# A token mixer with experts on one core: spans and exponentials of a step formed at the end of the step before, and four mixing deltas in one pass

## The chip, the cores and the metric

The kernel runs on one core of a Trainium2 chip, in float32. The metric is the device time of one execution in microseconds. Three runs of the kernel before gave 6115.89, 6119.67 and 6131.08 us; the median is 6119.67.

## The reference, cut to what matters

The first layer is a recurrent token mixer over x of shape (2, 4096, 512) with 16 heads of 32 channels; the second routes the 8192 rows to 8 experts by balanced assignment and runs a two-layer feed-forward net in each. The change touches the mixer alone.

```python
xx  = xprev - x
mix = tanh((x + xx * time_maa_x) @ time_maa_w1.T).reshape(B, T, 4, -1)
deltas = einsum('btfd,fcd->fbtc', mix, time_maa_w2)               # four of them, from 32 channels each
xrg, xwa, xk, xv = x[None] + xx[None] * (time_maa + deltas)
r = xrg @ receptance.T ; k = xk @ key_w.T ; v = xv @ value.T ; ...  # gates, decay w, kk, a, b = -kk * a
def step(S, inp):                                                 # over T, for each head, S is 32 x 32
    sab = einsum('bhvk,bhk->bhv', S, kk_)
    S = S * exp(w_)[:, :, None, :] + sab[..., None] * b_[:, :, None, :] + v_[..., None] * k_[:, :, None, :]
    y = einsum('bhvk,bhk->bhv', S, r_)
    return (S, y)
```

Then y is normed per head, a bonus is added, the gate multiplies, and `output` projects it.

## The kernel before, in words

**Tiles and chunks.** A tile is 64 tokens of each of the two sequences, 128 columns; channels lie on partitions in four groups (G). There are 64 tiles. The recurrence is solved in chunks of 32 tokens: in a chunk, queries (`kkn` and `r`) meet keys (`b` and `k2`), each weighted by an exponential of a difference of summed log-decays (`csum`). The difference is taken in blocks of 8 tokens against a reference in the block: `query_span` writes it into `dq` for all queries, `key_span(j)` into the second half of `keys` for the keys that block j can see, 128 to 512 wide (j = 0 to 3). ACT takes the exponentials in place (`exp_of_queries`, `exp_of_keys`), POOL multiplies them with `kkn` and `r` (`queries_u`, `queries_y`), DVE with `b` and `k2` (`make_keys`).

**Stages of a tile.** A tile passes five stages in successive steps: N loads its rows and norms them; A transposes x, mixes it, projects it and forms decays and keys; B forms the products of queries and keys (scores `u0` to `u5`, `y0` to `y5`), masks them into `raw`, and projects the values; C inverts the triangular systems by doubling (`inverse_stage`, k = 1, 2, 4, 8, 16), and passes the state through the two chunks; D norms, gates and projects the output. One `step` runs A of tile d + 3 and B of tile d + 2 beside C and D of older ones, so all of them are interleaved on each engine. Of 68 steps 28 are written out in a loop that runs twice, the others stand before and behind it.

**What sets the order.** The order is written by hand, one list per engine (`DVE_STEPS`, `ACT_STEPS`, `POOL_STEPS`, `PE_STEPS`, lines 255 to 274) that names every operation as stage.name, and the calls at the end of `on_vector`, `on_scalar`, `on_gpsimd` and `on_tensor` in the same order. Each operation adds one to its engine's semaphore of the step, and a consumer waits for a count (`dve["A.scan"]` of this step, `dve.ago(...)` of the step before). An engine runs its own list in order: whatever stands behind a waiting instruction waits too. Engines may run apart by less than two steps (`enter`, and `on_sync`, which issues all DMAs).

**PSUM.** Eight banks are shared in turns (`BANK`, line 275). Before a product is written, `clear` waits for the reader of the tenant before: delta0 in bank 3 follows `rated` (read by DVE as `A.rated`), delta3 in bank 2 follows `value` (read by ACT as `B.v`), score u3 follows u1 in bank 5 and u5 follows u3.

**PE's head of a step** before: transposes of x, value (0,2), first inverse stage (128 matmuls of 32 x 32), centring, mixing (needs `xxx`), router scores, value (2,3), variance, second stage (128), deltas 0 to 2, value (3,4), gate of the output, `gate1` (needs `xf0`), bonus, half of stage 4, `low_wa` (needs `xf1`), the other half, delta 3, score u0, stage 8 with `low_k` between its halves, score u1, key projection.

**Lines that matter.** L358 `query_span`, L363 `key_span`, L369 and L372 `make_keys`, L387 masks, L402 and L408 lerp and `xf`, L415 transposes between inverse stages, L426 `turn_z`, L430 to L436 the state, L443 `rated`, L504 `D.acc`, L531 the scan, L550 `xx`, L553 `xxx`; on PE L992 projections, L1001 low-rank products, L1025 inverse stages, L1040 scores, L1094 deltas, L1117 transposes of x, L1127 centring, L1134 mixing, L1188 the second low-rank pass; on POOL L902 `grow_of`, L914 `rk`.

## Time and profile before

| what | value |
|---|---|
| median of three runs | 6119.67 us |
| the profiled execution's own time | 6134.68 us |
| its span | 6132.7 us |
| PE busy | 5583.4 us (91%) |
| DVE busy | 3823.3 us (62%) |
| ACT busy | 1982.8 us (32%) |
| POOL busy | 1368.9 us (22%) |

All durations come from one profiled execution. The mixer takes the span's first 4180 us or so, the routing and the experts the rest. Busy time of PE counts matmuls from start to modelled end; a wait is put down to what released it, and "issue" stands where nothing that the profile shows did.

### The profile page before, as it was taken

How to read it: one execution, taken by the hardware profiler on the slowest of the kernel's cores; microseconds unless marked ns; L12 is line 12 of the kernel's file. 1: busy time of each engine (PE TensorE's matmuls, PEld its weight loads, DVE VectorE, ACT ScalarE, POOL GpSimd, SP SyncE). 2: the span in 40 equal slices, each digit the busy share in tenths (PEclk: the TensorE clock that was granted, in tenths of full speed). 3: DMA queues.
4: the chain of work that ended last, by engine and by line, in shares of the span. 5: the costliest groups of instructions: out<-in, count | busy, mean ns of one | idle time of the engine just before them, and what ended most of it. 6: DMA issues, size and time to landing. Idle time of an engine off the chain costs nothing. (4 is left out here: it accounts for less than half of the span.)

```text
span 6132.7 us, 244823 instructions
## 1 busy us (share of the span) xinstructions
PE 5583.4 (91%) x111176; PEld 3878.1 (63%) x111176; DVE 3823.3 (62%) x9004; ACT 1982.8 (32%) x3595; POOL 1368.9 (22%) x1156
## 2 busy tenths in 40 slices
PE   6989999898998998988999899883999999999998
PEld 5777777777777777777777777762444444444443
DVE  5887887888788787787887887874322332332310
ACT  3444444444444444444444444431100000000000
POOL 1222222222222222222222222221220220220220
PEclk9999999999999999999999999995999999999999
DMA  1000001000010000000000000003021121211210
GB/s 59 23 17 19 23 18 24 17 22 20 17 24 18 20 22 17 24 17 19 23 17 23 19 18 23 17 16 99 21 77 62 59 75 62 70 65 62 71 62 14
DMA packets 108641, 211.14 MB, mean 34 GB/s; under 512 B 25552, under 2 KB 26704, under 8 KB 107088
## 3 DMA queue, kind: packets, MB, share of 16 engines
q1 hardware_dynamic: 92240, 144.91, 8.1%
q0 software_dynamic: 15360, 50.48, 2.5%
q8 instruction: 882, 14.45, 1.0%
q14 instruction: 159, 1.30, 0.1%
HBM read 144.60 MB, written 50.72 MB: 32 GB/s over the span
## 5 line engine op out<-in xcount | busy, mean ns | idle before, releaser
L387 DVE COPY_PREDICATED time_raw<-time_known,w_bank 128x96 f32<-128x96 int32 (+6 forms) x3072 | 831.5, 275 | 337.3 <-PE w_bank L1040 245.2
L1850 PE MATMUL moe_bank<-moe_w,moe_hidden 128*128 128x512 f32 x2048 | 928.7, 596 | 0.0
L1837 PE MATMUL moe_bank<-moe_hT,moe_w 128*128 128x512 f32 x2048 | 923.4, 594 | 0.8 <-DVE moe_hT L1737 0.8
L1758 ACT ACTIVATE moe_hidden<-moe_bank,moe_b 128x512 f32<-128x512 f32 x256 | 175.9, 687 | 1628.1 <-PE moe_bank L1837 1628.1
L1837 PEld LDWEIGHTS moe_bank<-moe_hT,moe_w 128*128 128x128 f32 x2048 | 386.4, 190 | 471.3 <-issue 470.1
L1850 PEld LDWEIGHTS moe_bank<-moe_w,moe_hidden 128*128 128x128 f32 x2048 | 379.4, 190 | 429.5 <-issue 428.1
L902 POOL TENSOR_TENSOR time_grow<-time_eye,time_grow 128x512 f32<-128x512 f32 x256 | 340.4, 1330 | 1036.7 <-DVE time_grow L415 1036.7
L1025 PE MATMUL w_bank<-time_ew,time_grow 32*32 32x64 f32 x32768 | 413.1, 221 | 59.6 <-issue 36.1
L1025 PEld LDWEIGHTS w_bank<-time_ew,time_grow 32*32 32x32 f32 x32768 | 348.0, 105 | 170.1 <-issue 88.2
L1040 PE MATMUL w_bank<-time_keys,time_queries_u 32*32 32x160 f32 x8192 | 361.9, 304 | 31.5 <-issue 30.6
L1737 DVE COPY moe_hT<-moe_bank 128x512 f32<-128x512 f32 x64 | 44.2, 690 | 535.5 <-PE moe_bank L1824 535.5
L658 ACT COPY time_ew<-w_bank 128x1024 f32<-128x1024 f32 x192 | 194.4, 1012 | 563.0 <-DVE time_grow L415 562.9
L1040 PE MATMUL w_bank<-time_keys,time_queries_y 32*32 32x160 f32 x8192 | 329.7, 297 | 16.5 <-DVE time_mixed L504 12.1
L1040 PEld LDWEIGHTS w_bank<-time_keys,time_queries_y 32*32 32x32 f32 x8192 | 233.5, 105 | 110.1 <-issue 47.4
L402 DVE SCALAR_TENSOR_TENSOR time_lerp<-w_bank,time_maa,time_xx 128x128 f32<-128x128 f32 x1024 | 281.5, 337 | 10.8 <-PE w_bank L1094 10.6
L1040 PEld LDWEIGHTS w_bank<-time_keys,time_queries_u 32*32 32x32 f32 x8192 | 239.8, 106 | 75.8 <-issue 38.6
L992 PE MATMUL w_bank<-time_xf,time_value 128*128 128x128 f32 x2048 | 281.8, 287 | 1.3 <-issue 1.2
L992 PE MATMUL w_bank<-time_xf,time_key_w 128*128 128x128 f32 x2048 | 279.7, 291 | 3.3 <-issue 3.2
L992 PE MATMUL w_bank<-time_xf,time_receptance 128*128 128x128 f32 x2048 | 281.8, 287 | 0.0
L992 PEld LDWEIGHTS w_bank<-time_xf,time_key_w 128*128 128x128 f32 x2048 | 253.1, 201 | 39.6 <-issue 38.7
L1792 POOL DMA_INDIRECT out<-moe_result,moe_slots x64 | 68.6, 1071 | 922.9 <-DVE moe_result L1747 908.6
L1109 PE MATMUL w_bank<-time_output,time_mixed 128*128 128x512 f32 x512 | 257.5, 626 | 12.2 <-DVE time_by_values L494 4.1
(225 smaller groups left out, 9551.4 us busy)
## 6 DMA issues: line engine op xcount, KB each, us to landing
moe_w<-in_w SPq DMA_DIRECT2D x64, 1024.0 KB, 7.4
mid_xn<-time_xn_rows SPq DMA_DIRECT2D x128, 129.0 KB, 2.6
time_x_rows<-in_x SPq DMA_DIRECT2D x128, 128.0 KB, 2.7
time_base<-in_x SPq DMA_DIRECT2D x128, 128.0 KB, 3.3
mid_acc<-time_mixed SPq DMA_DIRECT2D x128, 128.0 KB, 2.6
mid_scores<-time_rated SPq DMA_DIRECT2D x128, 2.0 KB, 1.8
moe_b<-in_b SPq DMA_DIRECT2D x8, 256.0 KB, 12.7
time_receptance<-in_w_receptance SPq DMA_DIRECT2D x1, 1024.0 KB, 5.0
```

The source lines that it names most:

```text
L387: e.copy_predicated(by_raw[:, "uy".index(q), n0:n1, :, 0:8 * j + 8], known[:, "uy".index(q), :, :, mine].to_broadcast([P, n1 - n0, 2, 8 * ...
L402: e.scalar_tensor_tensor(grp(lerp, g), grp(BANK[f"delta{f}"], g), wt["maa"][:, f * G + g:f * G + g + 1], grp(xx, g), ALU.add, ALU.mult).th ...
L658: e.copy(col(got["ew"]), inv_bank).then_inc(act.sem, act.step(f"C.S{k}"))
L902: e.tensor_tensor(chunks(grow), every_unit(wt["eye2"]), chunks(grow), ALU.subtract).then_inc(pool.sem, pool.step(f"C.b{k}"))
L992: mm = e.matmul(ps[:, o * P:(o + 1) * P], weight[:, g * width + o * P:g * width + (o + 1) * P], rhs_of(g), start=g == 0 and (o == 0 or not ...
L1025: mm = e.matmul(both_banks[to, n * 2 * N + taken.start:n * 2 * N + taken.stop], by[rows, blk(n)], got["ew"][rows, n * 2 * N + taken.start: ...
L1040: mm = e.matmul(BANK[f"{q}{m}"][head(h), (n - n0) * 2 * KEYS:(n - n0 + 1) * 2 * KEYS], queries[q][head(h), blk(n)], keys[head(h), n * 2 * ...
L1109: mm = e.matmul(BANK["out"][:, :], grp(mixed, g), wt["output"][:, g * C:(g + 1) * C], start=g == 0, stop=g == G - 1)
L1758: e.activation(hidden[now % 4][:, :], up[now % 3][:, :], ACT.Gelu_apprx_tanh, bias=b1[:, x * FC + k:x * FC + k + 1]).then_inc(act.sem, act ...
L1792: e.indirect_dma_start(dram["out"], slot(x, t), tile(result, t), None).then_inc(core.stored, 16)
L1837: got = e.matmul(up[now % 3][:, :], w1[:, g * F + k * P:g * F + (k + 1) * P], hT[x % 2][:, g * CAP + half * HALF:g * CAP + (half + 1) * HA ...
L1850: got = e.matmul(down[t][:, :], hidden[now % 4][:, t * P:(t + 1) * P], tile(w2, k), start=k == 0, stop=k == FC - 1)
```

## The change

Spans and exponentials of tile t were formed at the start of the step in which B works on it; they are now formed at the end of the step before, in which A has just made `csum`. So their steps are called A.dq, A.dk3 to A.dk0, A.eq, A.ek3, A.ek012, and their readers in B wait for the step before. The scan is moved ahead (`summed_decay`), the product `b` is split off from it (`unit_gates`). The last delta joins the other three, behind the whole value projection. Orders are rearranged on all four engines.

```diff
@@ on_vector
             def query_span():
-                if "B.shrink" in act.was:
-                    e.wait_ge(act.old, act.ago("B.shrink"))
-                    e.wait_ge(pool.old, pool.ago("B.qy"))
-                e.tensor_tensor(by_block(dq), refs, spans, ALU.subtract).then_inc(dve.sem, dve.step("B.dq"))
+                if Bs:
+                    e.wait_ge(act.sem, act["B.shrink"])
+                    e.wait_ge(pool.sem, pool["B.qy"])
+                e.wait_ge(dve.sem, dve["A.scan"])
+                e.tensor_tensor(by_block(dq), refs, spans, ALU.subtract).then_inc(dve.sem, dve.step("A.dq"))
             def key_span(j):
-                if j == 3 and "B.y5" in pe.was:
-                    e.wait_ge(pe.old, pe.ago("B.y5"))
+                if j == 3 and Bs:
+                    e.wait_ge(pe.sem, pe["B.y4"])
+                    e.wait_ge(dve.sem, dve["B.bT"])
...
             def make_keys(j):
-                e.wait_ge(act.sem, act["B.ek3" if j == 3 else "B.ek012"])
+                e.wait_ge(act.old, act.ago("A.ek3" if j == 3 else "A.ek012"))
...
             def lerp_of(f):
-                if f == 3:
-                    e.wait_ge(pe.sem, pe["A.delta3"])
...
+            def unit_gates():
                 e.wait_ge(act.sem, act["A.tna"])
                 e.wait_ge(dve.sem, dve["A.kkn"])
...
@@ on_gpsimd
             def queries_u():
-                e.wait_ge(act.sem, act["B.eq"])
+                e.wait_ge(act.old, act.ago("A.eq"))
@@ on_tensor
             def scored():
                 clear(e, "rated")
+                e.wait_ge(act.sem, act["A.x"])
...
             def deltas():
-                for f in range(3):
+                for f in range(4):
                     clear(e, f"delta{f}")
                 e.wait_ge(act.sem, act["A.mix"])
-                delta_of(0, 1, 2).then_inc(pe.sem, pe.step("A.delta"))
-
-            def last_delta():
-                clear(e, "delta3")
-                delta_of(3).then_inc(pe.sem, pe.step("A.delta3"))
+                delta_of(0, 1, 2, 3).then_inc(pe.sem, pe.step("A.delta"))
```

The orders after, as the lists have them (a part of each):

```
DVE  A.xx A.xxx0-3 C.t1 A.rated B.kb3 B.kk3 B.kb2 B.kk2 B.kb1 B.kk1 B.kb0 B.kk0 N.stats N.mv A.lerp00-03 A.xf0 C.t2 D.normed ...
     A.xf3 B.u2 B.vT B.kT B.bT B.u3 N.shift ... B.u4 B.u5 B.ub A.min B.y0 B.y1 C.z0 B.y2 B.y3 A.scan A.wmk A.g1 A.p2 A.fk A.kkn
     D.acc C.rows0 C.shrunk0 C.state0 A.dq B.y5 B.y4 C.z1 A.dk3 A.dk2 A.dk1 A.dk0 A.b A.k2 C.rows1 C.shrunk1 C.state1
ACT  A.carried A.x D.squares C.S1 A.mix B.v D.lnv ... B.shrink A.lp A.lns N.ln2 C.u0 A.rs N.rs2 C.y0 A.decayed A.eq C.u1
     A.ek3 A.ek012 A.r C.y1
POOL B.rk C.b1 B.qu C.b2 C.b4 C.faded0 C.b8 B.qy B.e1 B.us A.lt C.faded1 B.ys
PE   A.x C.S1 A.scored D.centre A.mix B.value D.var A.delta C.S2 D.gate A.gate1 B.bonus A.low_wa C.S4 B.u0 B.u1 A.low_k C.S8
     C.S16 B.u2 ... (the rest as before)
```

In PE's list value (2,3) stands between centring and mixing, value (3,4) behind mixing. In the order before, DVE had `B.vT B.kT B.bT` ahead of the masks of y3, `A.kkn` behind the first state, the four factors (`A.wmk A.g1 A.p2 A.fk`) behind `C.z1`, and `A.scan A.b A.k2` behind the masks of y5; ACT had `C.u0` ahead of `A.lp`; POOL had `B.qy` behind `C.b2` and `A.lt` ahead of `B.us`.

## Rows read from the trace of the kernel before

**Rows 1.** Page: busy us of engines; instruction queue: fetches, MB, share.

```profile
PE 5583.4 (91%) x111176; PEld 3878.1 (63%) x111176; DVE 3823.3 (62%) x9004; ACT 1982.8 (32%) x3595; POOL 1368.9 (22%) x1156
...
q8 instruction: 882, 14.45, 1.0%
```

**Rows 2.** Stretch of 24 steps; busy us of each engine (instructions), granted clock, DMA.

```profile
2094.00:3634.00 1540.00, 1398.91 (x39791) 1131.92 (x39790) 1227.97 (x3000) 671.80 (x1248) 378.61 (x312) 0.97 0.08 20
```

**Rows 3.** PE's waits in that stretch; idle us in total, times, longest.

```profile
PE w_bank L1001 <- DVE time_xf L408: 44.5, 36, 2.0
PE w_bank L1025 <- issue: 30.4, 23, 2.4
PE w_bank L1094 <- DVE time_rated L443: 13.1, 16, 0.8
PE w_bank L1134 <- DVE time_lerp L553: 12.9, 16, 0.9
PE w_bank L1040 <- issue: 10.5, 8, 2.2
PE w_bank L1025 <- ACT time_hid_w L728: 5.5, 24, 0.3
```

**Rows 4.** Order of time, one step; start, us, engine, line, [idle before <- releaser].

```profile
2929.04 0.66 PE L1117 MATMUL w_bank<-time_ident,time_xn_rows 128*128 128x128 f32 x4
...
2931.41 1.29 PE L1025 MATMUL w_bank<-time_ew,time_raw 32*32 32x32 f32 x128
...
2932.61 0.69 DVE L550 TENSOR_TENSOR time_xx<-time_x 128x512 f32<-128x512 f32 x1
2932.62 1.13 PE L1127 MATMUL w_bank<-time_yT,time_centre 128*128 128x512 f32 x2
...
2934.62 1.13 PE L1134 MATMUL w_bank<-time_lerp,time_maa_w 128*128 128x128 f32 x8 [0.87 <-DVE time_lerp L553]
...
2940.75 1.17 PE L1094 MATMUL w_bank<-time_mix,time_maa_w 32*128 32x128 f32 x24 [0.83 <-DVE time_rated L443]
...
2945.02 0.69 DVE L408 TENSOR_TENSOR time_xf<-time_lerp,time_x 128x512 f32<-128x512 f32 x1
...
2945.86 1.13 PE L1001 MATMUL w_bank<-time_xf,time_gate_w 128*128 128x128 f32 x8 [1.96 <-DVE time_xf L408]
...
2951.39 1.15 PE L1094 MATMUL w_bank<-time_mix,time_maa_w 32*128 32x128 f32 x8
...
2968.78 1.17 PE L1188 MATMUL w_bank<-time_hid,time_low_w 32*128 32x128 f32 x32 [0.23 <-ACT time_tail L749]
```

**Rows 5.** The same step, spans on DVE and POOL beside them.

```profile
2934.39 0.75 DVE L358 TENSOR_TENSOR time_dq<-time_csum 128x576 f32<-128x576 f32 x1
...
2936.29 2.14 DVE L363 TENSOR_TENSOR time_keys<-time_csum 128x384 f32<-128x384 f32 x3
...
2936.45 1.50 POOL L902 TENSOR_TENSOR time_grow<-time_eye,time_grow 128x512 f32<-128x512 f32 x1 [4.62 <-DVE time_grow L415]
```

**Rows 6.** The same step, its end, and the start of the next.

```profile
2982.35 0.69 DVE L504 TENSOR_TENSOR time_mixed<-w_bank,time_base 128x512 f32<-128x512 f32 x1 [2.13 <-PE w_bank L1109]
...
2987.62 0.45 DVE L426 STREAM_TRANSPOSE time_rhs<-w_bank 128x256 f32<-128x256 f32 x1 [1.70 <-PE w_bank L1067]
...
2992.42 0.66 PE L1117 MATMUL w_bank<-time_ident,time_xn_rows 128*128 128x128 f32 x4
...
2995.52 0.42 DVE L436 TENSOR_TENSOR time_state<-time_grown,time_faded 128x256 f32<-128x256 f32 x1
```

**Rows 7.** Order of time on PE, a wait by issue in another step.

```profile
2546.13 1.27 PE L1025 MATMUL w_bank<-time_ew,time_raw 32*32 32x32 f32 x127
...
2549.45 0.25 PE L1025 MATMUL w_bank<-time_ew,time_raw 32*32 32x32 f32 x1 [2.05 <-issue]
2549.63 2.08 PE L1127 MATMUL w_bank<-time_yT,time_centre 128*128 128x512 f32 x2
```

**Rows 8.** Stretch behind that wait, columns as in rows 2.

```profile
2549.00:2552.00 3.00, 2.55 (x6) 1.46 (x7) 3.00 (x6) 0.26 (x1) 0.83 (x1) 0.51 0.02 5
```

More of the change, by code:

```diff
@@ L255, in time_mix @@
         DVE_STEPS = (
[8 rows of a table removed]
-            "C.state1").split()
[7 rows of a table added]
+            "B.y5.2 B.y5.3 B.y4.0 B.y4.1 B.y4.2 B.y4.3 C.z1 A.dk3 A.dk2 A.dk1 A.dk0 A.b A.k2 C.rows1 C.shrunk1 C.state1").split()
         ACT_STEPS = (
-            "A.carried A.x D.squares B.ek3 C.S1 A.mix B.ek012 B.eq D.lnv N.lnv D.rstd N.rstd C.S2 B.v D.affine0 D.affine1 "
-            "D.affine2 D.affine3 C.S4 A.hid_g A.hid_w A.hid_a C.S8 A.hid_kkk A.hid_mk C.S16 A.k A.exp_z A.tail A.tna A.tnma "
-            "A.thmk A.sq N.xn B.e0 B.decay_end B.shrink C.u0 A.lp A.lns N.ln2 A.rs N.rs2 C.y0 C.u1 A.decayed A.r C.y1").split()
+            "A.carried A.x D.squares C.S1 A.mix B.v D.lnv N.lnv D.rstd N.rstd C.S2 D.affine0 D.affine1 D.affine2 D.affine3 "
+            "C.S4 A.hid_g A.hid_w A.hid_a C.S8 A.hid_kkk A.hid_mk C.S16 A.k A.exp_z A.tail A.tna A.tnma A.thmk A.sq N.xn "
+            "B.e0 B.decay_end B.shrink A.lp A.lns N.ln2 C.u0 A.rs N.rs2 C.y0 A.decayed A.eq C.u1 A.ek3 A.ek012 A.r C.y1").split()
         POOL_STEPS = (
-            "B.rk C.b1 B.qu C.b2 B.qy C.b4 C.faded0 C.b8 B.e1 A.lt B.us C.faded1 B.ys").split()
+            "B.rk C.b1 B.qu C.b2 C.b4 C.faded0 C.b8 B.qy B.e1 B.us A.lt C.faded1 B.ys").split()
         PE_STEPS = (
-            "A.x C.S1 D.centre A.mix A.scored D.var C.S2 A.delta B.value D.gate A.gate1 B.bonus A.low_wa C.S4 A.delta3 B.u0 "
-            "A.low_k C.S8 B.u1 C.S16 B.u2 A.key B.u3 A.decay B.u4 B.u5 A.low2 B.y0 B.y1 A.sums C.z0 B.y2 B.y3 C.u0 C.y0 "
-            "D.out B.y5 B.y4 C.z1 C.u1 A.recept C.y1").split()
+            "A.x C.S1 A.scored D.centre A.mix B.value D.var A.delta C.S2 D.gate A.gate1 B.bonus A.low_wa C.S4 B.u0 B.u1 "
+            "A.low_k C.S8 C.S16 B.u2 A.key B.u3 A.decay B.u4 B.u5 A.low2 B.y0 B.y1 A.sums C.z0 B.y2 B.y3 C.u0 C.y0 D.out "
+            "B.y5 B.y4 C.z1 C.u1 A.recept C.y1").split()
         BANK = Banks(psum, [
@@ L683, in exp_of_queries @@
             def exp_of_queries():
-                e.wait_ge(dve.sem, dve["B.dq"])
-                e.activation(col(dq), col(dq), ACT.Exp).then_inc(act.sem, act.step("B.eq"))
+                e.wait_ge(dve.sem, dve["A.dq"])
+                e.activation(col(dq), col(dq), ACT.Exp).then_inc(act.sem, act.step("A.eq"))
             def mix_of():
@@ L826, in on_scalar @@
                 squares_of()
-            if Bs:
-                exp_of_keys("B.ek3", key_units(1, 3), "B.dk3")
             if Cs:
@@ L833, in on_scalar @@
             if Bs:
[L834 to L835 removed]
+                value_arrived()
             if D:
@@ L882, in on_scalar @@
                 y_of(0)
+            if A:
+                decayed_of()
+                exp_of_queries()
+            if Cs:
                 solved("u", 1)
             if A:
-                decayed_of()
+                exp_of_keys("A.ek3", key_units(1, 3), "A.dk3")
+                exp_of_keys("A.ek012", by_key[:, :, 1, 0:key_at(3)], "A.dk0")
+            if A:
                 recept_arrived()
@@ L1210, in on_tensor @@
                 inverse_stage(1, 1)
+            if A:
+                scored()
             if D:
                 centred()
+            if Bs:
+                value_of(2, 3)
             if A:
                 mix_of()
-                scored()
             if Bs:
-                value_of(2, 3)
+                value_of(3, 4).then_inc(pe.sem, pe.step("B.value"))
             if D:
                 var_of()
+            if A:
+                deltas()
             if Cs:
@@ L1222, in on_tensor @@
                 inverse_stage(2, 1)
-            if A:
-                deltas()
-            if Bs:
-                value_of(3, 4).then_inc(pe.sem, pe.step("B.value"))
             if D:
@@ L1248, in on_tensor @@
                 inverse_stage(8, 1)
-            if Bs:
-                score("u", 1)
             if A:
```

64 lines of the change are left out of this document (28 added, 36 removed), and 15 rows, old and new, of the table DVE_STEPS.

## The prediction

> **What bounds the kernel now.** I read the page first, then the stretches, TensorE's waits, and one step of the loop in order of time. The page has PE busy for 91% of the span, more than any other engine [rows 1]. The stretches show the same for the part that the change touches: in 2094 to 3634 us PE is busy for 1398.9 us of 1540, DVE for 1228 [rows 2]. One wait there, that of the second inverse half for ACT, occurs once a step and stands there 24 times [rows 3], so a step is 1540/24 = 64.2 us, PE works 58.3 of them and idles 5.9. Behind that part the routing and the experts run, which the change doesn't touch. So the time before comes down only where a PE wait goes or PE's own work shrinks, and both count about 61 times (56 full steps of 64, the filling and draining ones in part).
>
> The waits [rows 3], a step: for `xf0` and `xf1` 44.5/24 = 1.85 us, for `A.rated` 0.55, for `xxx` 0.54, for ACT before the second half of a stage 0.23. Those four, 3.17 us, stand in the first half of the step and end on DVE or behind it. "Issue" waits (30.4 + 10.5 and some small ones, near 47 in all) are 1.96 us a step; nothing of the program releases them. The other 0.8 us stand late in the step.
>
> The step in order of time says why DVE is late: the mixing matmuls wait 0.87 us for `xxx`, the deltas 0.83 for `A.rated`, and the first gate product 1.96 for `xf0`. That sum is formed at 2945.02, though its deltas were done at 2941.92 [rows 4]: DVE was busy in between, and before, with spans and products of keys [rows 5].
>
> **The change, part by part.**
>
> *One pass for four deltas.* The fourth delta alone, 8 matmuls, takes 1.15 us, 1.08 to the next start. Three together, 24 matmuls on three row groups, take 1.17, and the second low-rank pass, 32 matmuls on four row groups, takes 1.17 too [rows 4]. So the fourth rides free: -1.08 us of PE work a step. Its cover is `B.v`: bank 2 must be read by ACT before. `B.v` now stands before the logs, and value's last part ends one `var` matmul (1 us) before the deltas; ACT's copy takes 0.6. Price if that cover is gone: a few tenths.
>
> *Spans and exponentials moved.* At the head DVE loses `dq` 0.75, `dk3` 0.7 (of `kb3`'s size) and the three others, 2.14 us together [rows 5]: 3.5 us. Of the 2.14 some 1.1 are no work: `C.b1` on POOL runs 1.50 us beside them [rows 5]. That cost moves, it doesn't vanish: `b1` will meet `kb3`. `qu`, which meets `kb2` now, will follow `b1` at once and meet `kk3`. DVE takes from `xx` at 2932.61 to the end of `xf0` at 2945.71 13.1 us [rows 4]; less 3.5, plus 1.1 for `b1`, 10.7. It will start at 2.3 us into the step (its tail is shorter, next part), where now it starts at 3.6, so `xf0` is there at 13.0. PE takes from its first transpose at 2929.04 to the gate product at 2945.86 16.82 us, of them 3.66 waits [rows 4]: 13.2 without, in the new order too, which has the same work ahead of that product. In the same way `xf1` comes 3.1 us behind `xf0`, and PE wants it 3.1 us behind the first; `qy` is moved behind `b8` and no longer meets it. So the four waits go: -3.17, with DVE hardly ahead.
>
> *The end of the step.* Behind `z1` DVE had factors, masks, scan, `b`, `k2`: the state add ends 3.5 us after PE's next step has begun, 2995.94 against 2992.42 [rows 6]. In the new order the four key spans (3.5 less `dq` less the 1.1: 1.7), `b` and `k2` (1.3) follow `z1`, 3.0 us. Before, `z1` ends at 2988.07, 7.9 us before the add [rows 6], of which the three operations of the state take 2.3 (one blocked by `rk`) and the rest 5.6. So `rows1` will wait for PE instead, and the add will end near 2.3 (`rk` on POOL may meet it, as it does now). `scan`, four factors and `kkn` (512 wide; 0.69 and 0.75 are the rows of that width, the scan I take at 1.3), some 4.2 us, now stand between the masks of `y3` and `D.acc`. There is the idle time of 2.13 us before `D.acc` [rows 6], plus the three transposes of 0.6 to 0.7 moved away from there: 4.0. `D.acc` is 0 to 0.3 us late, and score `y4` waits for it. The transposes now stand before the masks of `u3`, for whose bank score `u5` waits: 0 to 0.5 late in steps that PE runs through. On ACT `ek3` and `ek012` stand before `A.r`, which POOL's next `rk` wants, and before `C.y1`, which the next first stage wants 2.4 us into the step; both have over 1 us in hand. `dq` waits for `B.shrink` and `B.qy`, long done; `dk3` for score `y4`, done 3 us before. Nothing queued behind them is late. `A.lp`, which the scan needs, no longer stands behind `C.u0` and comes earlier by ACT's wait for it. SP issues the same DMAs; the scores leave earlier. For all these places I take +0.2 a step, bounds 0 and 0.8.
>
> *What a fuller PE meets: "issue".* In a step with such a wait the run of 128 small matmuls on `raw` breaks: it ran 127 in 1.27 us, then stood 2.05 us [rows 7]. In the step of [rows 4] the 128 run through in 1.29. Followed through the 24 steps, the break moves back by 16 matmuls a step and returns every eighth; it is there 31 times [rows 3], in the first stage or in the last one and score `u2`. The page counts 882 fetches of instructions for 2 x 111176 instructions [rows 1], one for 252, that is for 126 matmuls with their weight loads. I read the break as a dense run that outpaces the next fetch: where such a block of about 126 is used up too soon, PE stands. Slow 128-wide matmuls and waits refill. In the new order the 32 deltas run straight into the 128 of the second stage, 160 in 2.6 us, where now a wait of 0.83 us parts them; `u0`, `u1` and the first half of stage 8 make 112 in 2.9 us; and `scored` (16) follows the first stage. Bounds: nothing (the fetch keeps up as now), and 2.0 us for about 1.3 boundaries a step more, 2.6. Nearest are the two dense runs of now, which make most of the 1.96 us: two more such stretches, not quite as dense, +1.55.
>
> The Trainium skill (Runtime: NRT & Kernel Launch, Instruction fetch mechanics) says that instructions stream in 16 KiB blocks of 256 and that their fetch is hidden since the engine dispatches slower than blocks arrive. The trace agrees with the block size, 252, and not with the hiding, 2.05 us. By that rule this term is nothing and the sum -4.05 a step.
>
> *Half clock.* Behind the 2.05 us break the granted clock is 0.51 over 3 us, which is 1.2 GHz of the two levels [rows 8]: the two centring matmuls behind it took 2.08 us [rows 7], where they take 1.13 at full clock [rows 4], so that it cost 0.95 in them and at most 1.5 (half of the 3 us) in all. The mean clock of the 24 steps is 0.97 [rows 2], so some 6% of them, 3.9 us a step, are at half. Of the new breaks about 0.35 a step should be long: +0.4, bounds 0 and 1.3 x 1.5 = 2.0.
>
> **Sum.** -1.08 - 3.17 + 0.2 + 1.55 + 0.4 = -2.1 us a step, x 61 = -128. The profiled execution took 6134.7 us (span 6132.7 and 2.0 around it), 15.0 above the median 6119.7; so 6007 in its terms and 5992 in those of the median. I say 5995.
>
> **Rivals.**
> (A) The forecast, 2.1 us a step, 1.2 to 3.0 with its terms: 5935 to 6045.
> (B) Fetches stay hidden. Gain 1.08 + 3.17 - 0.2 = 4.05 a step, 247 us: 5873; with half of it true, to 5935. For it: in the steps of now the second stage, as dense as the first, shows no break at all. Against: a wait follows it now. It is what the rule of the Trainium skill (Runtime: NRT & Kernel Launch, Instruction fetch mechanics) would give.
> (C) The waits change places: DVE, 1228 us busy of 1540 before, has 13 us a step in hand in sum but under 0.3 at `xf0`, `xf1`, `u3`, `D.acc`. If each collision with POOL costs another 1.2 us, or the scan meets one, PE waits 2.5 to 4 us again at those places and only the pass is left: with the fetch term nothing or little, gain 0 to 1.2: 6045 to 6120. For it: four places with no slack. Against: each late place also relieves the next and the fetch.
> (D) Slower: breaks and half clock eat it. The place is the second stage and the run `u0`, `u1`, stage 8. It takes 2.6 us of breaks, each of 1.3 followed by a half clock at 1.5 us: +2.6 + 2.0 + 0.2 - 4.25 = +0.55 a step, 34 us: 6154. It decides from the point where breaks and half clock together pass 4.05 us a step. For it: PE is already at half clock behind breaks of 2 us. Against: DVE's lateness absorbs some of the breaks, and the short ones need not draw the half clock.
>
> **How the numbers follow.** A 0.57, B 0.19, C 0.15, D 0.09. Likeliest 5995; A's own range 5935 to 6045. The range of 8 in 10 takes most of B and C: 5895 to 6085. What a measurement here can tell from no change is 0.3%, 18 us. Faster: A, B and half of C, 0.83; within: 0.08; slower: D with a bit of C, 0.09.
>
> **What would show it.** In the trace after, per step: no wait for `xf0` or `xf1` over 0.2 us; deltas one group of 32 at 1.2 us; DVE idle before `rows1`, not PE before `xxx`; "issue" waits up from 1.96 to about 3.5, the new ones in the second stage and in `u1` or stage 8; PE's mean clock no higher. Wrong if "issue" stays at 2 (then B), if PE waits for DVE over 1.5 us a step (C), or if PE's busy time a step grows in spite of 8 fewer serial matmuls (D).

## The result and the profile after

The changed kernel took 5988.91 us, the median of 4 runs (5982.03 to 5994.03), the kernel before beside it 6121.32 (6115.89 to 6131.08). The ratio is 0.9781, 95% interval 0.9764 to 0.9798: 2.2% faster. 5995 was predicted, so the time was right within some 6 us. The steps behind it were not all right, and the experiments say which.

The page of the kernel after, busy time of each engine; the second line is the instruction queue:

```profile
PE 5480.1 (92%) x111176; PEld 3819.9 (64%) x111176; DVE 3758.0 (63%) x9004; ACT 1986.1 (33%) x3595; POOL 1405.8 (23%) x1156
...
q8 instruction: 882, 14.45, 1.0%
```

A stretch of exactly 24 steps of the kernel after; columns as in [rows 2]:

```profile
2035.04:3507.76 1472.72, 1349.33 (x39793) 1101.81 (x39793) 1202.81 (x3001) 672.74 (x1248) 392.70 (x313) 0.99 0.09 21
```

1472.72/24 is 61.4 us a step, where it was 64.2. TensorE works 56.2 of them in place of 58.3, and idles 5.1 in place of 5.9.

TensorE's waits over some 24 steps (2024 to 3500 us) of the kernel after, as in [rows 3]:

```profile
PE w_bank L1024 <- issue: 64.3, 55, 2.9
PE w_bank L1024 <- ACT time_hid_w L727: 10.4, 19, 0.7
PE w_bank L1039 <- issue: 8.6, 9, 2.0
PE w_bank L1024 <- POOL time_grow L902: 6.5, 23, 0.3
PE w_bank L1039 <- DVE time_mixed L503: 6.2, 25, 0.3
PE w_bank L1076 <- issue: 5.8, 6, 1.3
...
PE w_bank L1000 <- DVE time_xf L407: 2.8, 7, 0.7
```

The waits for `xf0` and `xf1` went from 44.5 us to 2.8; those for `xxx` and `rated` have no line left. In their place stand 64.3 us of "issue" in the inverse stages, where 30.4 stood, and twice the wait that the trace puts down to `hid_w` (10.4 in place of 5.5). The wait of 6.5 us for POOL's `grow` is new; it stands ahead of stage 16, where score `u1` stood before.

One step of the kernel after, in order of time on TensorE:

```profile
2715.18 0.66 PE L1116 MATMUL w_bank<-time_ident,time_xn_rows 128*128 128x128 f32 x4
...
2717.56 1.29 PE L1024 MATMUL w_bank<-time_ew,time_raw 32*32 32x32 f32 x128
...
2721.45 1.06 PE L1133 MATMUL w_bank<-time_lerp,time_maa_w 128*128 128x128 f32 x8
...
2724.33 1.26 PE L1093 MATMUL w_bank<-time_mix,time_maa_w 32*128 32x128 f32 x32
2725.52 1.22 PE L1024 MATMUL w_bank<-time_ew,time_grow 32*32 32x64 f32 x103
2728.32 0.43 PE L1024 MATMUL w_bank<-time_ew,time_grow 32*32 32x64 f32 x25 [1.57 <-issue]
2728.68 1.16 PE L991 MATMUL w_bank<-time_hid_g,time_gate_w 128*128 128x128 f32 x8
...
2733.42 0.85 PE L1024 MATMUL w_bank<-time_ew,time_grow 32*32 32x64 f32 x64
2734.08 1.83 PE L1039 MATMUL w_bank<-time_keys,time_queries_u 32*32 32x160 f32 x48
2736.52 0.91 PE L1024 MATMUL w_bank<-time_ew,time_grow 32*32 32x64 f32 x64 [0.61 <-ACT time_hid_w L727]
...
2741.57 1.21 PE L1024 MATMUL w_bank<-time_ew,time_grow 32*32 32x32 f32 x121 [0.28 <-POOL time_grow L902]
2745.00 0.26 PE L1024 MATMUL w_bank<-time_ew,time_grow 32*32 32x32 f32 x7 [2.23 <-issue]
```

No product waits for VectorE. The four deltas are one group of 1.26 us, the second stage behind them breaks after 103 matmuls, and so does stage 16 after 121. From the first break to the second there are 506 matmuls, by the groups of this step (the omitted ones too), with as many weight loads; with the waits and signals between them that is 1024 instructions, four times 256. The kernel after has 75 breaks of over 1 us between 600 and 3600 us; of the 74 distances from one to the next, counted in the trace's TensorE records (matmuls, weight loads, semaphore instructions), 73 are multiples of 256 to within one.

VectorE in the same step and at the end of it:

```profile
2716.86 0.42 DVE L435 TENSOR_TENSOR time_state<-time_grown,time_faded 128x256 f32<-128x256 f32 x1
2717.32 0.69 DVE L550 TENSOR_TENSOR time_xx<-time_x 128x512 f32<-128x512 f32 x1
...
2720.56 1.65 DVE L373 TENSOR_TENSOR time_keys<-time_keys,time_k 128x512 f32<-128x512 f32 x1
2722.13 1.55 DVE L370 TENSOR_TENSOR time_keys<-time_keys,time_b 128x384 f32<-128x384 f32 x1
...
2727.47 0.69 DVE L407 TENSOR_TENSOR time_xf<-time_lerp,time_x 128x512 f32<-128x512 f32 x1
...
2772.52 1.66 DVE L364 TENSOR_TENSOR time_keys<-time_csum 128x512 f32<-128x512 f32 x4
...
2776.93 0.45 DVE L429 STREAM_TRANSPOSE time_grown<-w_bank 128x256 f32<-128x256 f32 x1 [1.55 <-PE w_bank L1085]
```

`kk3` and `kb2` take 1.65 and 1.55 us beside POOL's `b1` (from 2719.89, 1.77 us) and `qu` (from 2721.62, 1.64 us); `kb3`, of the size of `kk3`, takes 0.68 just before, and `kk2`, of the size of `kb2`, 0.56 behind `qu`. VectorE waits for TensorE before `rows1` (1.55). `xf0` ends 13.0 us into the step.

The table gives sums of the traces' records over the 56 full steps, in us a step ("half clock" is time at a granted clock below 0.9, busy or idle; "other" is all of TensorE's idle time but issue). All kernels of the next section but fetch_alone are in it; the last column is the ratio of the times to the kernel before. The records are of one profiled execution each. That of the kernel before took 13 us more than the median of its runs, which is 0.2 us a step, and that of pass_and_again 17 us less; the others lie within 9 us of theirs.

| kernel | step | TensorE busy | issue | other | half clock | ratio |
|---|---|---|---|---|---|---|
| before | 64.03 | 58.14 | 2.04 | 3.83 | 3.17 | 1 |
| after | 61.68 | 56.47 | 3.56 | 1.64 | 2.38 | 0.9781 |
| pass_alone | 64.63 | 57.35 | 2.36 | 4.90 | 4.14 | 1.0083 |
| spans_alone | 61.16 | 57.43 | 2.45 | 1.27 | 2.44 | 0.9721 |
| split_stage2 | 61.89 | 56.80 | 3.26 | 1.81 | 2.19 | 0.9786 |
| early_wait | 62.75 | 57.10 | 4.05 | 1.59 | 3.78 | 0.9873 |
| pass_and_again | 61.47 | 57.24 | 3.05 | 1.17 | 2.38 | 0.9780 |
| split_stage16 | 60.49 | 57.02 | 1.91 | 1.55 | 0.61 | 0.9646 |
| u1_back | 60.50 | 56.97 | 2.33 | 1.19 | 1.22 | 0.9651 |
| both_places | 60.36 | 57.23 | 1.60 | 1.51 | 0.85 | 0.9631 |
| both_with_pass | 61.34 | 56.35 | 2.45 | 2.54 | 1.65 | 0.9728 |
| split16_with_pass | 61.10 | 56.25 | 2.89 | 1.94 | 0.98 | 0.9728 |
| values_later | 60.14 | 57.29 | 1.73 | 1.10 | 0.91 | 0.9612 |

### The profile page after: what moved, and what is told of

Read it like the earlier page. It is cut to its first block and busy times, and to the rows that moved or that the text cites. A ratio compares the mean times of both kernels' runs of the same rounds, so it can differ in the third digit from the quotient of the medians.

```text
span 5987.6 us, 244885 instructions
## 1 busy us (share of the span) xinstructions
PE 5480.1 (92%) x111176; PEld 3819.9 (64%) x111176; DVE 3758.0 (63%) x9004; ACT 1986.1 (33%) x3595; POOL 1405.8 (23%) x1156
## 5 line engine op out<-in xcount | busy, mean ns | idle before, releaser
L388 DVE COPY_PREDICATED time_raw<-time_known,w_bank 128x96 f32<-128x96 int32 (+6 forms) x3072 | 815.3, 274 | 234.9 <-PE w_bank L1039 148.7
L1024 PE MATMUL w_bank<-time_ew,time_grow 32*32 32x64 f32 x32768 | 426.3, 217 | 201.6 <-issue 146.2
L991 PE MATMUL w_bank<-time_xf,time_key_w 128*128 128x128 f32 x2048 | 295.0, 302 | 6.2 <-issue 6.0
L1039 PEld LDWEIGHTS w_bank<-time_keys,time_queries_u 32*32 32x32 f32 x8192 | 252.5, 107 | 69.8 <-issue 38.4
L414 DVE STREAM_TRANSPOSE time_grow<-w_bank 128x512 f32<-128x512 f32 x256 | 182.9, 714 | 174.8 <-PE w_bank L1024 174.8
L991 PEld LDWEIGHTS w_bank<-time_xf,time_key_w 128*128 128x128 f32 x2048 | 268.7, 211 | 32.6 <-issue 26.9
L991 PEld LDWEIGHTS w_bank<-time_xf,time_value 128*128 128x128 f32 x2048 | 256.9, 197 | 33.1 <-issue 32.8
```

The lines of the kernel that those rows point to most:

```text
L388: e.copy_predicated(by_raw[:, "uy".index(q), n0:n1, :, 0:8 * j + 8], known[:, "uy".index(q), :, :, mine].to_broadcast([P, n1 - n0, 2, 8 * ...
L414: e.transpose(chunks(grow), rest_of(both_banks)).then_inc(dve.sem, dve.step(f"C.t{k}"))
L991: mm = e.matmul(ps[:, o * P:(o + 1) * P], weight[:, g * width + o * P:g * width + (o + 1) * P], rhs_of(g), start=g == 0 and (o == 0 or not ...
L1024: mm = e.matmul(both_banks[to, n * 2 * N + taken.start:n * 2 * N + taken.stop], by[rows, blk(n)], got["ew"][rows, n * 2 * N + taken.start: ...
L1039: mm = e.matmul(BANK[f"{q}{m}"][head(h), (n - n0) * 2 * KEYS:(n - n0 + 1) * 2 * KEYS], queries[q][head(h), blk(n)], keys[head(h), n * 2 * ...
```

## The experiments

**1. The pass alone (pass_alone).** The kernel before, with its spans where they were:

```diff
-A.x C.S1 D.centre A.mix A.scored D.var C.S2 A.delta B.value D.gate ... C.S4 A.delta3 B.u0
+A.x C.S1 D.centre A.mix A.scored B.value D.var C.S2 A.delta D.gate ... C.S4 B.u0
-                delta_of(0, 1, 2).then_inc(pe.sem, pe.step("A.delta"))
+                delta_of(0, 1, 2, 3).then_inc(pe.sem, pe.step("A.delta"))
```

On ScalarE `B.v` stands before `D.lnv`.

> The kernel before with one part of the change: value projection finished ahead of the variance, the copy of the values moved up on ScalarE, four deltas in one pass; spans and exponentials stay at the head of their step. Theory (parts add, each by its own mechanism): the pass saves 1.08 us of TensorE's work a step, and the waits for VectorE at xxx and xf0 stay (xf0 still stands behind the spans and products, which end at 14.9 us into the step). Gain 1.0 us a step, 61 us: 6060, ratio 0.990. Rival (the pass is only worth something once VectorE is early, since TensorE then waits longer for xf0): the wait for xf0 and xf1 grows from 1.85 us to 2.5 or more and the gain is under 0.4 us a step, 6097 to 6121.

Measured: 6177.31 us (6173.35 to 6189.14), ratio 1.0083, interval 1.0064 to 1.0102. Both expectations missed; this kernel is slower by 0.6% to 1.0%. Its waits, over 24 steps (2100 to 3660 us):

```profile
PE w_bank L998 <- DVE time_xf L406: 50.1, 32, 2.3
PE w_bank L1022 <- ACT time_hid_w L726: 34.0, 24, 1.5
```

The wait before stage 8, 5.5 us in [rows 3], is 34.0 here: 1.4 us in every step. What it is, experiment 6 shows. The run holds a little more than the pass: the value projection ends earlier too, and the wait for `rated`, 13.1 us in [rows 3], has no line.

**2. The spans alone (spans_alone).** The changed kernel with the last delta behind stage 4 as before:

```diff
-D.gate A.gate1 B.bonus A.low_wa C.S4 B.u0 B.u1 A.low_k C.S8
+D.gate A.gate1 B.bonus A.low_wa C.S4 A.delta3 B.u0 B.u1 A.low_k C.S8
```

> The kernel after without the pass: three deltas together, the fourth alone behind stage 4, the rest of the new order kept. Theory: against the kernel before the waits for VectorE (3.17 us a step) go, the issue waits rise by 1.3 to 1.6; net 1.2 to 1.6 us a step, 6025 to 6048, ratio 0.985 to 0.988; issue waits about 3.3 us a step. Rival (most of the gain of the whole is the pass): 6080 or more.

Measured: 5957.61 us (5949.39 to 5964.17), ratio 0.9721, interval 0.9707 to 0.9736; it missed low by 67 us. Less than the whole change gives more: the pass costs 31 us on top of the spans by the medians, 37 by the ratios. In the table it saves 0.96 us of work a step and brings 1.1 of issue and 0.4 of other waits. Most of the issue arises at two places. Breaks of over 0.5 us, summed over the 56 steps, make 0.02 us a step in the second stage without the pass and 0.78 with it, and 0.10 and 0.40 in stage 8.

**3. Is it the dense run behind the pass? (split_stage2, early_wait).** The first puts the output's gate, 128-wide matmuls, between the halves of the second stage:

```diff
                 inverse_stage(2, 0)
-                inverse_stage(2, 1)
             if D:
                 gate_of()
+            if Cs:
+                inverse_stage(2, 1)
```

> The kernel after with the gate product of the output, 8 wide matmuls of 1.05 us, between the two halves of stage 2 instead of behind both; nothing else differs. Theory (a dense run of small matmuls outpaces the fetch of instructions): the issue waits in stage 2 (0.78 us a step in the kernel after) fall by about 0.4 to 0.5, so 25 to 30 us less than the kernel after: 5960. Rival (the breaks are tied to places in the code, not to density): the same sum of issue waits, 5985 to 5995. Second rival: stage 2 ends 1 us later for VectorE's transpose and ScalarE's copy, and stage 4 waits for it: 0.3 us a step more at stage 4, which eats the gain.

Measured: 5998.40 us (5991.84 to 6008.64), ratio 0.9786. Nothing gained: issue falls by 0.3 us a step, and the bonus product waits for VectorE 17 times in 24 steps (5.3 us), where it did twice. By place, the breaks in the second stage fall from 0.78 to 0.19 us a step and those in stage 4 rise from 0.23 to 0.46: the break moves on to the next run. Breaking up this place isn't enough.

The second puts a wait that is met by the time TensorE gets there ahead of the first stage:

```diff
                         e.wait_ge(pool.old, pool.ago("B.e1"))
+                        if A:
+                            e.wait_ge(act.sem, act["A.x"])
```

> The kernel after with one more wait: the first inverse stage waits for A.x on ScalarE, which ends 1.7 us into the step, 0.6 us before TensorE reaches that stage. Theory (the fetch of the next block starts only when the sequencer, held by a wait, runs on; the first stage waited for C.y1 until 2.1 us into the step in the kernel before, and since the change only until 0.9): the issue waits in the first stage grow from 0.29 us a step towards the 0.79 of the kernel before, half clock more often, +0.4 to 0.7 us a step, 6013 to 6030. Rival: a wait that is met before TensorE gets there costs nothing: 5989, issue waits in the first stage 0.3.

Measured: 6054.86 us (6047.48 to 6060.06), ratio 0.9873: the direction of the theory, and twice its size. The wait itself never shows in TensorE's idle time. Issue rises by 0.5 us a step, half clock by 1.4, and the breaks in the first stage are mostly 1.7 to 2.1 us again, where the kernel after mostly has 0.6 to 1.1. The theory behind the experiment, that a sequencer held by a wait can't run ahead and so meets the fetch late, agrees with it; no record shows the sequencer's own place. The three kernels line up: TensorE reaches the first stage 2.37 us into the step in all of them (medians), the last thing that it waits for there ends at 2.17 in the kernel before, at 0.89 in the kernel after and at 1.74 in early_wait, and the first stage's breaks make 0.78, 0.28 and 0.61 us a step.

**4. The pass, and the fourth delta again where it was (pass_and_again).** spans_alone with four deltas in the pass, the fourth being computed a second time behind stage 4:

```diff
-                delta_of(0, 1, 2).then_inc(pe.sem, pe.step("A.delta"))
+                delta_of(0, 1, 2, 3).then_inc(pe.sem, pe.step("A.delta"))
```

> All four deltas in one pass as in the kernel after, and the fourth computed once more behind stage 4, where the kernel before had it (the same values, 1.08 us of TensorE's work a step that nothing needs); its reader waits for the second. Theory now (measured: the pass cost 31 us on top of the spans, though it took 0.96 us of work from TensorE a step; the 8 wide matmuls behind stage 4 gave the fetch of instructions and the copy of stage 4 the time that they need anyway): useless work in that place makes the kernel after no slower, and issue waits fall from 3.6 to about 2.5 us a step; 5950 to 5975. Rival (the pass itself costs, by four row groups at once or by its wait for the copy of the values): the time is that of the kernel after plus the added work or part of it, 5990 to 6050.

Measured: 5992.27 us (5975.05 to 6006.50), ratio 0.9780, interval 0.9764 to 0.9796: as fast as the changed kernel (0.9781) though it does 0.8 us more work a step. The theory's 5950 to 5975 missed; the time lies at the foot of the rival's range, where none of the added work is paid for. So the eight serial matmuls behind stage 4 cost nothing where they stand. With them back, the breaks in stage 8 fall from 0.40 to 0.07 us a step. Those in the second stage stay (0.83), and they are what is left to spans_alone: issue 3.05 against 2.45.

What can hold up the fetch at the second stage? The pass brings more than eight matmuls. It must wait for ScalarE's copy of the values, since the fourth delta's bank is that of `value`. That copy in the kernel after, in the step shown above:

```profile
2723.49 0.58 ACT L719 COPY time_v<-w_bank 128x512 f32<-128x512 f32 x1 [0.67 <-PE w_bank L991]
```

The same place in spans_alone, without the pass:

```profile
2698.25 0.59 ACT L721 COPY time_v<-w_bank 128x512 f32<-128x512 f32 x1 [0.67 <-PE w_bank L993]
...
2698.95 1.17 PE L1095 MATMUL w_bank<-time_mix,time_maa_w 32*128 32x128 f32 x24
...
2700.04 1.32 PE L1026 MATMUL w_bank<-time_ew,time_grow 32*32 32x64 f32 x111
2701.52 0.35 PE L1026 MATMUL w_bank<-time_ew,time_grow 32*32 32x64 f32 x17 [0.15 <-issue]
```

With the pass the copy ends at 2724.07 and the deltas start at 2724.33; in nearly all of the 56 steps their first weight load starts 0.22 us behind the copy's end, and TensorE idles for some 0.08 us, too short for the list of waits. Without it the deltas have no idle time before them and start by themselves. So with the pass a wait releases TensorE right ahead of the dense run, as early_wait does by design. And without it 24 deltas and 128 matmuls of the second stage run through, with 0.15 us of break after 111, where 32 deltas and the same stage break for 1.57. Eight matmuls more in the run, or the wait ahead of it: no run separates the two.

**5. Dense runs elsewhere (split_stage16, u1_back, both_places).** Three kernels without the pass. One has the key projection's second part between the halves of the last inverse stage, one has score `u1` behind stage 8 as in the kernel before, one has both:

```diff
-                inverse_stage(16, 0)
-                inverse_stage(16, 1)
+                inverse_stage(16, 0); key_of(2, 3); inverse_stage(16, 1)     # split_stage16
-B.u0 B.u1 A.low_k C.S8 C.S16
+B.u0 A.low_k C.S8 B.u1 C.S16                                               # u1_back
```

> The kernel spans_alone (spans and exponentials moved, three deltas together, the fourth alone) with one of the four parts of the key projection (8 wide matmuls, 1 us) between the halves of stage 16. Theory (a run of 128 small matmuls and the scores behind it outpace the fetch): issue waits in stage 16 and score u2, some 1.2 us a step there, fall by 0.3 to 0.6; 5920 to 5945 against 5958. Rival (a wide group of 1 us is too short a pause, as between the halves of stage 2, where the issue waits fell by only 0.3 us and the time rose by 9 us): 5955 to 5970.

> The kernel spans_alone with score u1 behind stage 8, where the kernel before had it, instead of ahead of it. Theory (u0, u1 and the first half of stage 8 make a dense run of 112, and u1 there covers the wait for the copy of stage 4): two effects of opposite sign; the wait for the copy comes up by 0.2 to 0.3 us a step, the dense run ahead of stage 8 goes, but u1 comes to stand nearer to stage 16: 5950 to 5985, most likely 5970. Rival (the place of u1 is what made spans_alone fast): 6000 or more.

> The kernel without the four-row pass (deltas three and one), with the key projection's second part between the halves of the last inverse stage and score u1 behind stage 8 as in the kernel before. Each of the two alone gave 41 to 44 us over the spans alone (5957.6). Theory (both act on the same cause, dense runs that meet the fetch and the half clock behind the breaks, of which 1.9 and 2.3 us of issue and 0.6 and 1.2 us of half clock a step were left): the gains overlap, issue falls to 1.5 a step, half clock to 0.4, the new wait for shift stays: 5880 to 5905, most likely 5893. Rival (they act on different things and add): 5870 to 5877. Rival (the key projection is needed late in either order, and u1 behind stage 8 makes a dense run of it with the first half of stage 16, so that one undoes the other): 5910 to 5930.

Measured: 5916.73 us (ratio 0.9646, interval 0.9632 to 0.9660), 5914.08 (0.9651, 0.9638 to 0.9664) and 5906.46 (0.9631, 0.9618 to 0.9644). The first came out 3 us beyond the expected range. The second was expected to lose, or at best to gain 8 us, and gained 44. The expectation's dense run of `u0`, `u1` and stage 8 is not where it comes from: the breaks in stage 8 rise from 0.10 to 0.17 us a step. What changes is stage 16. With `u1` ahead of it again the wait for POOL's product (6.5 us in spans_alone) has no line, and the breaks in stage 16 are 1.2 us in the middle in place of 2.3. The first move shortens the same breaks, 1.2 in place of 2.3, and those in score `u2` behind them (0.41 to 0.12 us a step). In both the time at half clock falls the most, from 2.44 to 0.61 and 1.22 us a step, and TensorE's busy time with it. Together they gain hardly more than either, which fits one cause. Part of it is another thing: with the key projection moved, score `u5` waits for VectorE (`shift`), 12.4 and 12.8 us in 24 steps, 0.5 us a step, and experiment 8 goes after that.

**6. The pass on these (both_with_pass, split16_with_pass).** Is the pass a loss by itself, and by what? The diffs are those of experiment 5 on the changed kernel.

> The same two moves on the changed kernel, with its one pass for four deltas. It tells whether the pass is a loss by itself. Theory (the pass costs because it and the missing matmuls behind stage 4 make denser runs; the two moves relieve the later ones but not the run of deltas and second stage): it stays slower than the kernel without the pass by 10 to 25 us, issue 2.3 to 2.8 a step in place of 1.5: 5900 to 5920. Rival (most of the pass's cost was in u1 and stage 8 and in stage 16, where the head of the step was too short): with these relieved the pass gives its 0.96 us of work a step less the second stage's breaks, and the kernel is equal to the other or up to 25 us faster: 5865 to 5895.

> The changed kernel, with its pass and with u1 ahead of stage 8, and with the key projection's second part between the halves of stage 16. Its pair is the same kernel without the pass (5916.7). The pass with u1 behind stage 8 cost 59 us (5965.7 against 5906.5), of them 1.07 us a step a wait of stage 8 for ScalarE's copy of stage 4: the fourth delta behind stage 4 had covered that copy. Theory (the pass's price is that cover, and breaks): with u1 in its place the copy is covered but for 0.4 us, so that the pass costs 0.4 of that wait and 0.9 of breaks less 0.96 of its work a step, +10 to +35 us: 5927 to 5952. Rival (cover is all of it): breaks don't rise, 0.96 gained less 0.4: 5880 to 5900.

Measured: 5965.71 us (ratio 0.9728, interval 0.9715 to 0.9741), 59 us above its pair and outside both expectations, and 5955.12 (0.9728, 0.9712 to 0.9744), 38 us above its pair by the medians and 50 by the ratios, where +10 to +35 was expected. In both the breaks of the second stage make 0.78 or 0.79 us a step, as in the changed kernel. The order of time of both_with_pass shows the part that I had missed:

```profile
2165.35 0.64 PE L1024 MATMUL w_bank<-time_ew,time_grow 32*32 32x64 f32 x39 [0.59 <-issue]
...
2165.80 1.02 PE L1039 MATMUL w_bank<-time_keys,time_queries_u 32*32 32x160 f32 x24
2166.03 0.72 DVE L414 STREAM_TRANSPOSE time_grow<-w_bank 128x512 f32<-128x512 f32 x1 [1.36 <-PE w_bank L1024]
...
2166.78 1.01 ACT L657 COPY time_ew<-w_bank 128x1024 f32<-128x1024 f32 x1 [3.77 <-DVE time_grow L414]
2166.83 1.27 POOL L902 TENSOR_TENSOR time_grow<-time_eye,time_grow 128x512 f32<-128x512 f32 x1 [5.04 <-DVE time_grow L414]
...
2168.24 0.84 PE L1024 MATMUL w_bank<-time_ew,time_grow 32*32 32x64 f32 x64 [1.43 <-ACT time_hid_w L727]
```

Stage 4 ends at 2165.99; VectorE transposes its result (0.72), POOL multiplies it (1.27, to 2168.10) beside ScalarE's copy, and stage 8 starts at 2168.24. From the end of stage 4 to the start of stage 8 that takes 2.25 us; it takes as long in the kernel after (2734.27 to 2736.52) and in both_places below (2197.33 to 2199.59), with other work on TensorE in between. `hid_w`, which the trace names, merely ended last on ScalarE. In between TensorE has only `u0` here. With the fourth delta there, as in both_places, the same chain leaves TensorE's next weight load 0.52 us of idle time, and its matmuls 4.8 us in 24 steps, 0.2 a step:

```profile
2196.62 0.71 PE L1026 MATMUL w_bank<-time_ew,time_grow 32*32 32x64 f32 x47 [0.95 <-issue]
...
2197.26 1.15 PE L1095 MATMUL w_bank<-time_mix,time_maa_w 32*128 32x128 f32 x8
...
2198.34 1.24 PE L1041 MATMUL w_bank<-time_keys,time_queries_u 32*32 32x160 f32 x24
...
2199.55 0.96 PEld L1026 LDWEIGHTS w_bank<-time_ew,time_grow 32*32 32x32 f32 x64 [0.52 <-ACT time_hid_w L729]
2199.59 1.17 PE L1026 MATMUL w_bank<-time_ew,time_grow 32*32 32x64 f32 x64
```

The delta's 1.15 us were cover for work that TensorE has to wait for anyway. The changed kernel has `u1` there in its place, and a wait of 0.61 us stays (before 2736.52 in its step above). And `u1` is then missing ahead of stage 16, where the wait for POOL's product and the longer breaks of experiment 5 stand.

**7. The fetch by itself (fetch_alone).** The changed kernel with 4096 matmuls of the second stage's shape in straight line behind the mixer, with no wait among them and no other engine at work:

```diff
+        for again in range(32):
+            for n in range(16):
+                for h in range(HG):
+                    nc.tensor.matmul(both_banks[head(h), n * 2 * N:(n + 1) * 2 * N], grow[head(h), blk(n)],
+                                     handed[0]["ew"][head(h), n * 2 * N:(n + 1) * 2 * N], start=True, stop=True,
+                                     skip_group_check=True)
```

> The kernel after with 4096 matmuls of 32 x 32 by 64 (with their weight loads, as in stage 2) in a straight line behind the mixer, when all other engines are idle; their result goes nowhere. In the steps 128 of them take 1.25 to 1.5 us when they run through. Theory (the fetch of instructions bounds a dense run): TensorE breaks once per 128, one such group takes 3.0 to 3.7 us, all 32 take 96 to 118 us. Rival (the breaks come from something else in the step, as data transfers or semaphores): 40 to 50 us in all, without breaks.

One run, 6122.74 us. These matmuls, their idle time, and their stretch:

```profile
L1338 PE MATMUL w_bank<-time_ew,time_grow x4096: 211/214/311, 4075.1 to 4188.6; 32*32 32x64 f32 x196
its engine sat idle before it (us, times) until:
  issue: 46.4, 30
```

```profile
4075.00:4189.00 114.00, 67.30 (x4096) 62.39 (x4096) 0.00 (x0) 0.00 (x0) 0.00 (x0) 0.96 0.02 5
```

113.5 us for 32 groups of 128 matmuls and 128 loads: 3.55 us for each 256 instructions, with 30 breaks of 1.55 us, at a mean granted clock of 0.96 (1.00, the upper level, for most of it). The matmuls wait for no semaphore, so I read this as the rate at which instructions arrive. In the loop 128 such matmuls run in 1.7 to 1.8 us (64 take 0.85 to 0.91), twice as fast.

**8. The next wait (values_later).** both_places with the transpose of v, 0.70 us on VectorE, moved away from ahead of the masks of `u3`, for which score `u5` waited 12.8 us in 24 steps:

```diff
-B.u2.3 B.vT B.kT B.bT B.u3.0 ... B.y1.3 C.z0
+B.u2.3 B.kT B.bT B.u3.0 ... B.y1.3 B.vT C.z0
```

> The kernel without the pass and with both moves (the third measured at 5906.5), and the transpose of v (0.70 us on VectorE) moved from ahead of the masks of u3 to ahead of z0, where VectorE stands idle for 1.4 us. Theory (score u5 waits 12.8 us of 24 steps, 0.53 us a step, for VectorE's masks of u3, whose three transposes stand before them): that wait goes, 0.53 x 61 = 32 us less some of it to breaks by a fuller TensorE: 5875 to 5892. Rival (z0 is late by the transpose and scores y2 and u0 of the state behind it wait in its place, or the fetch takes it): 5900 to 5915.

Measured: 5888.88 us (5878.22 to 5900.54), ratio 0.9612, interval 0.9598 to 0.9626. Other waits fall from 1.51 to 1.10 us a step and issue gives 0.13 of it back. By the ratios it gains some 12 us, in intervals that overlap, by the medians 18: the wait went and the time lies inside the theory's range, but only a third to a half of the forecast 32 us came. It is the fastest kernel of the study, 3.9% below the one before and 1.7% below the changed one.

## Why the prediction was right in sum and wrong in its parts

**The waits for VectorE: right.** 3.17 us a step were to go; those before `xxx`, `rated` and `xf1` did, 0.1 us before `xf0` stay. `xf0` was forecast at 13.0 us and ends at 13.03 (median). `state1` was forecast near 2.3 us into the step and ends at 2.1 (median). POOL's `b1` took its toll on `kk3` rather than on `kb3`, and `qu` on `kb2` rather than on `kk3`. In spans_alone the waits other than issue fall from 3.83 to 1.27 us a step.

**One pass for four deltas: wrong, and by its sign.** The term was -1.08 us, "the fourth rides free". The work does fall by 0.8 to 0.96 us a step. But in four pairs the kernel with the pass is slower: by 48 us on the kernel before, 31 on the spans, 38 to 50 and 59 on the better orders, +0.5 to +1.0 us a step. The step that failed is the question of cover. I asked what covers `B.v`, and not what the delta behind stage 4 itself covers: the 2.25 us chain of VectorE, POOL and ScalarE to stage 8, whose remaining wait of 0.23 stands in [rows 3]. The other part is fetch, and which part is larger depends on the order. Where `u1` stands behind stage 8 (pass_alone, both_with_pass), the pass brings 1.0 to 1.1 us a step of other waits, and 0.3 and 0.85 of issue. Where `u1` has taken the delta's place (the changed kernel, split16_with_pass), it brings 0.4 of other waits and 1.0 to 1.1 of issue. Of that the prediction had the second stage in its issue term, but even with it the pass was to gain. Its "price if that cover is gone: a few tenths" looked at idle time alone: the wait for `B.v` shows only 0.08 us of that, and what it may cost by the break behind it is in experiment 4.

**The end of the step: near.** +0.2 was taken, bounds 0 and 0.8. `D.acc` costs 0.24 us a step, where it cost 0.19 before, and `rows1`, `y5` and `u5` are not late. The output projection's waits for VectorE (0.15) went, so the end of the step as a whole costs no more than before. The waits before stages 8 and 16, 0.5 us a step more, are not of the end of the step: they come by the orders of the pass and of `u1`.

**Issue: the size right, half of its places wrong.** 1.96 to about 3.5 a step was forecast, 2.04 to 3.56 is measured. The spans, which take the waits away, account for 0.4 of it (2.45), the pass for 1.1. By place (breaks of over 0.5 us, a step), +1.55 was taken for the second stage and for `u0`, `u1` and stage 8. The second stage breaks in 27 of 56 steps by 1.2 to 2.2 us, 0.78 where nothing was, and stage 8 went from 0.11 to 0.40: 1.07 together. Stage 16 went from 0.30 to 0.72 and stage 4 from nothing to 0.23, and the first stage fell from 0.78 to 0.28, by its earlier inputs, as experiment 3 suggests. None of the three was forecast, and that they nearly cancel is luck. Experiment 7 shows that instructions can fail to keep up with a long run of such matmuls, with 3.55 us for 256 of them. It doesn't show why one place breaks and another as dense does not. The Trainium skill (Runtime: NRT & Kernel Launch, Instruction fetch mechanics) has the blocks of 256, and the distances of the breaks here (73 of 74) agree; it has the fetch as mostly hidden, and 46.4 us of idle time in 113.5 speak against that for small matmuls. A step has 26 x 128 matmuls and loads, 13 blocks, 46 us at that rate of 61: the supply suffices on average, and what is lost is lost in some dense runs.

**Half clock: the added part right, the sign of the whole wrong.** +0.4 was forecast; the time at half clock fell from 3.17 to 2.38 us a step. The mean clock of 0.97, read as 3.9 us a step at half clock, was a coarse reading: the records have 3.17. I put each such stretch of the traces down to the longest idle time of TensorE in the 6 us before it; the figures shift by some 0.2 with how such a rule is drawn. Behind issue waits there are 1.65 us a step before and 1.76 after. But behind the waits for `xf0` and `rated` there were 1.16 us a step, and with the waits these went; the rest has no long wait near it. The trace of before has in the step after that of [rows 4]

```profile
3009.23 1.48 PE L1001 MATMUL w_bank<-time_xf,time_gate_w 128*128 128x128 f32 x8 [1.96 <-DVE time_xf L408]
3010.50 1.92 PE L1171 MATMUL w_bank<-time_rk,time_bonus_ones 128*128 128x128 f32 x8
```

and behind it, in a stretch of 3 us with columns as in [rows 2],

```profile
3010.00:3013.00 3.00, 3.00 (x61) 2.77 (x60) 2.97 (x7) 2.78 (x6) 2.21 (x2) 0.50 0.00 0
```

which is 1.2 GHz: the same price as behind the break of [rows 7], on a wait that the change removes. It doesn't always come. In the step of [rows 4] a wait of the same length ends at 2945.86, and behind it stands

```profile
2946.00:2949.00 3.00, 2.91 (x80) 2.45 (x80) 2.97 (x7) 2.63 (x6) 2.44 (x2) 1.00 0.00 0
```

Of the 30 waits for `xf0` of 1.65 us and more, 17 have the half clock behind them. I had priced the half clock for breaks alone and forgot to credit it to the waits. The kernel after shows it behind its break at 2745.00:

```profile
2746.00:2749.00 3.00, 3.00 (x23) 2.51 (x16) 2.12 (x6) 0.00 (x0) 0.00 (x0) 0.53 0.02 5
```

**So** the sum, -2.1 us a step, measured -2.35 in the profiled executions (-2.2 by the medians, 132 us over 61), was right by offset, which is luck. Waits other than issue fell by 2.19, where -3.17 and +0.2 were taken: 0.8 too well, most of it before stages 8 and 16. TensorE's busy time fell by 1.67, where the pass and the half clock were taken at -1.08 and +0.4: 1.0 too little, since what runs at half clock is busy for longer. The sum of issue was right. Rival B's premise fell: fetches don't stay hidden. Of rival C some wait did change place, half a microsecond a step before stages 8 and 16, and not where it said. Rival D's mechanism is real, since early_wait loses 66 us by breaks and half clock alone, but the changed kernel is far from its 4.05 us.

What stays open: by what means a wait ahead of a dense run makes its break longer, and how much of the pass's 0.8 us a step of breaks in the second stage comes from its four row groups, from the 160 matmuls in line, and from its wait for `B.v`. None was measured by itself. For the wait speaks that breaks are long where the last thing waited for came late: in the first stage of the kernel before and of early_wait, in the second stage with the pass, in stage 16 behind the wait for POOL. Of these only early_wait changed the wait alone; for the others it is argued.

## What to carry to other kernels

Before moving or merging an operation on the engine that sets the time, ask what it covers: find the chain on the other engines that runs beside it, and compare that chain's length with the work left between its two ends. Eight serial matmuls that look wasteful may fill a gap that is there anyway. And once TensorE is over 90% busy with small matmuls, try to spread them: wide matmuls between the halves of stage 16 gave 41 us here, between those of stage 2 nothing. Look at what TensorE waits for right ahead of a dense run, even where the wait itself is too short to be seen, and count a change of order by the idle "issue" time as well as by the waits it takes away.

## What the runs showed of the hardware

In straight line, with no other engine at work, instructions reached TensorE at 256 in 3.55 us, 128 matmuls of 32 x 32 with their loads, which run in 1.7 to 1.8 us in the loop (fetch_alone). A wait already met ahead of such a run cost 66 us over the kernel (6054.86 against 5988.91). Idle times of TensorE of 1.65 us and more often had the half clock behind them, whatever ended them: in the 56 steps of the kernel before it stood behind 17 of the 23 longest issue breaks and behind 17 of the 30 waits for `xf0` of 1.65 to 1.98 us, and behind none of the 9 such waits of 1.5 to 1.65. In fetch_alone the granted clock was 1.00 from 4100 to 4125 us, with eight breaks of 1.55 us in these 25 us. Work taken off TensorE (0.8 to 1.0 us a step) made the kernel slower in all four orders tried.
